# One written order for every engine in a two-pass attention and feed-forward kernel

## The reference

```
q = layernorm(x) @ Wq + bq ; k = ctx @ Wk + bk ; v = ctx @ Wv + bv      # split in 16 heads
scores = q k^T / sqrt(8), -1e9 where mask == 0 ; probs = softmax(scores)
x = x + (probs v) @ Wo + bo
h = gelu(bitlinear(layernorm(x), w1)) ; x = x + bitlinear(h, w2)
# bitlinear: rows rounded to 8 bits by their own maximum, weights to -1, 0, 1 times a scale
```

## Time and profile before

| | us |
|---|---|
| median of 3 runs | 1119.72 |
| lowest and highest run | 1116.97, 1119.76 |
| the profiled execution | 1116.7 |
| its span, first to last instruction | 1115.0 |
| granted TensorE clock over the span | 0.981 |

### The profile page before, as it was taken

The page is one execution under the profiler, slowest core; times in us unless marked ns, Lnnn a source line. Parts: engine busy times, 40 slices in busy tenths (PEclk is TensorE's granted clock), DMA queues, the critical chain, the costliest instruction groups (busy, mean ns, idle before and its releaser), DMA issues.

```text
span 1115.0 us, 29461 instructions
## 1 busy us (share of the span) xinstructions
PE 992.6 (89%) x10188; PEld 753.8 (68%) x10188; DVE 756.1 (68%) x1796; ACT 637.0 (57%) x1176; POOL 260.0 (23%) x414
## 2 busy tenths in 40 slices
PE   3588899999999999999999999999999999999994
PEld 1266676777767677776767777677776767777673
DVE  3767676776767776776777667676767767676664
ACT  1254456565575656557565665656566566666553
POOL 5402222222202222221222222122222211222200
PEclk9689999999999999999999999999999999999997
DMA  6553255453445545344554544455554444554300
GB/s 141 138 134 75 66 137 132 111 123 93 113 108 136 134 110 123 97 105 109 134 134 114 122 102 106 106 128 134 118 121 106 106 106 122 134 126 106 82 17 5
DMA packets 74985, 123.09 MB, mean 110 GB/s; under 512 B 6016, under 2 KB 58960, under 8 KB 74960
## 3 DMA queue, kind: packets, MB, share of 16 engines
q1 hardware_dynamic: 72649, 121.47, 45.7%
q10 hardware_dynamic: 2311, 1.29, 0.5%
HBM read 37.22 MB, written 0.92 MB: 34 GB/s over the span
## 4 chain that ended last, share of the span: by engine, by line
PE 53%; issue 15%; ACT 14%; DVE 12%; ACTq 3%; DMA 3%; SPq 1%; DVEq 0%
PE ps_v L810 10%; PE ps_p L704 8%; PE ps_s L767 8%; DVE seg_max L994 8%; ACT probs L602 7%; PE ps_s L772 7%; PE ps_p L708 6%; PE ps_p L723 5%; ACT k_hi L582 3%; PE ps_p L716 2%; PE ps_p L718 2%; ACTq L594 2%; PE ps_p L701 2%; ACT vals L586 2%; DMA ctx_sb<-in_ctx_dram 1%
## 5 line engine op out<-in xcount | busy, mean ns | idle before, releaser
L994 DVE TENSOR_REDUCE seg_max<-ps_p 128x1 f32<-128x500 f32 x672 | 422.8, 670 | 117.7 <-PE ps_p L723 114.8
L602 ACT ACTIVATE probs<-ps_s 125x448 f32<-125x448 f32 x768 | 367.7, 545 | 80.0 <-PE ps_s L772 75.3
L767 PE MATMUL ps_s<-qry,keys 121*125 121x448 f32 x768 | 292.9, 388 | 37.0 <-ACT probs L602 33.5
L772 PE MATMUL ps_s<-qry,keys 128*125 128x448 f32 x768 | 280.0, 371 | 0.0
L723 PE MATMUL ps_p<-keys,qry 120*128 120x500 f32 x576 | 243.3, 473 | 12.9 <-DVE k_lo L981 5.2
L586 ACT ACTIVATE vals<-ps_p 125x512 f32<-125x512 f32 x96 | 57.6, 600 | 279.9 <-PE ps_p L708 279.9
L767 PEld LDWEIGHTS ps_s<-qry,keys 121*125 121x125 f32 x768 | 140.8, 187 | 76.2 <-ACT probs L602 57.0
L810 PE MATMUL ps_v<-probs,vals 125*32 125x112 f32 x6144 | 168.0, 261 | 0.9 <-ACT probs L602 0.8
L810 PEld LDWEIGHTS ps_v<-probs,vals 125*32 125x32 f32 x6144 | 144.9, 110 | 30.3 <-issue 30.3
L723 PEld LDWEIGHTS ps_p<-keys,qry 120*128 120x128 f32 x576 | 109.6, 191 | 79.4 <-DVE seg_max L994 33.0
L772 PEld LDWEIGHTS ps_s<-qry,keys 128*125 128x125 f32 x768 | 142.2, 188 | 14.6
(11 more groups left out here) (123 smaller groups left out, 757.6 us busy)
## 6 DMA issues: line engine op xcount, KB each, us to landing
keys<-k_hi SPq DMA_DIRECT2D x128, 375.0 KB, 5.0
keys<-k_lo SPq DMA_DIRECT2D x64, 375.0 KB, 7.0
ctx_sb<-in_ctx_dram SPq DMA_DIRECT2D x31, 750.0 KB
keys<-keys SPq DMA_DIRECT2D x32, 328.1 KB
mask_sb<-in_mask_Bx1xSxS_ik_dram SPq DMA_DIRECT2D x31, 328.1 KB
out_dram<-x_rows SPq DMA_DIRECT2D x16, 56.0 KB, 1.6
ctx_sb<-in_ctx_dram ACTq DMA_DIRECT2D x1, 750.0 KB
x_rows<-in_x_dram SPq DMA_DIRECT2D x1, 672.0 KB, 11.6
```

The lines of the kernel that those rows point to most:

```text
L602: act.activation(probs[:, c % NP, h], ps_s[0:KC, (2 * c + h) % NS, 0:HC], ACT.Exp)\
L767: return pe.matmul(ps_s[0:KC, (2 * c + h) % NS, 0:HC], keys1[0:ONE + 1, p, h, c * KC:(c + 1) * KC], qry1[0:ONE + 1, p, h, :], start=start, ...
L772: return pe.matmul(ps_s[0:KC, (2 * c + h) % NS, 0:HC], keys2[:, p, h, c * KC:(c + 1) * KC], qry2[:, p, h, :], start=start, stop=not start)
L994: dve.tensor_reduce(seg_max[:, m, s:s + 1], bank[:, 0:SEG], AX.X, ALU.max)\
```

## The change

SLOTS and the sequences derived from it are replaced by one written list per kind of pass, which every engine walks, taking the words that concern it. A word is a piece with its number, or a job of one engine: own (values taken from ps_v), rows and hid (quantisation), sum (mask sum on ScalarE), some, bias, neg (turn_max), shift (place_shift), norm, abs, and k, the VectorE part of K.

- Each score half is a word of its own, with maxima, K, T and others between single halves.
- s0 s1 move from the end of the pass before to its own start.
- T1 and T2 stand apart from T0; K0 comes after S11; in the even pass V1, F0 and V2 stand before R0, and R0 before P2; in the odd pass R0 before P2 and V2 after.
- bias_mask stands before VectorE's copy of R instead of after it; find_some moves later; F0 moves from chunk 5 to near the end of the pass.
- VectorE's k part stands apart from K, mostly behind maxima or rows.
- The mask sum follows S9 (even) or T1 (odd).
- Banks go round in order, without the exception for G; S of the weight sum is called Z.

```diff
-SLOTS = [
-    [("T", 0), ("T", 1), ("T", 2), ("M", 0), ("D", 0), ("M", 1)],
-    [("M", 2)],
-    [("M", 3)],
-    [("M", 4), ("V", 0)],
-    [("M", 5), ("M", 6), ("M", 7)],
-    [("F", 0), ("M", 8), ("M", 9)],
-    [("K", 0), ("M", 10), ("M", 11)],
-    [("M", 12), ("V", 1)],
-    [("K", 1), ("M", 13), ("M", 14), ("M", 15)],
-    [("K", 2), ("M", 16), ("M", 17)],
-    [("M", 18), ("M", 19)],
-    [("M", 20), ("R", 0), ("V", 2)],
-]
+EVEN = order("""
+    own T0 s0 s1 f0 f1 S2 M0 D0 M1 S3 S4 T1 M2 S5 S6 M3 S7 M4 M5 S8 M6 S9 sum S10 S11 M7 M8 M9 K0 O0
+    rows P0 S12 k0 S13 k1 K1 V0 some S14 T2 M10 S15 rows1 S16 M11 K2 M12 k2 P1 S17 M13 M14 S18 S19
+    M15 S20 M16 M17 M18 S21 S22 M19 S23 M20 V1 F0 shift neg V2 bias R0 P2
+""")
+ODD = order("""
+    T0 own T1 s0 H0 sum s1 M0 M1 M2 f0 f1 S2 M3 T2 M4 M5 S3 S4 S5 M6 M7 M8 S6 D0 S7 hid G0 S8 K0 P0
+    S9 M9 hid1 K1 S10 S11 k0 M10 k1 S12 M11 M12 S13 hid2 S14 M13 V0 K2 k2 M14 hid3 S15 S16 M15 S17
+    P1 some M16 U0 M17 F0 S18 S19 Y0 M18 S20 M19 S21 M20 S22 neg S23 V1 shift bias R0 P2 V2
+""")
...
+LEAD = ["T0 T1 T2 M0 M1 some F M2 M3 K0 M4 M5 k0 M6 M7 K1 M8 M9 k1 M10 M11 K2 M12 M13 k2",
+        "M14 M15 M16 M17 M18 M19 M20 neg R shift V0 V1 V2 bias norm2"]
...
+    "first_even": with_more(EVEN, {"S5": "X1", "S7": "Q2", "S9": "Q3 abs", "S11": "B", "k1": "X2", "S21": "Q4", "S23": "Q5",
+                             "M20": "Z"}, ahead=(0, 1, 2)),
+    "last_even": ahead_only(EVEN, (-1, 0, 1)),
+    "last_odd": ahead_only(ODD, (-1, 0)),
...
-    if ("G", 0) in slots and len(slots) > 12:
-        at = slots.index(("G", 0))
-        own = (at + 7 - len(slots)) % NBANK
-        for n in range(at + 1):
-            bank[slots[n]] = (own + n - at) % NBANK
-        for n in range(6):
-            bank[slots[at + 1 + n]] = (own + 1 + n % 3) % NBANK
...
+            def score(bt, j):
+                b, k, p = bt
+                c, h = divmod(j, 2)
+                wait(pe, exp_done, 2 * NC * b + j - NS + 1)
+                first_pass(bt, c, h, True)
+                second_pass(bt, c, h, False).then_inc(scores_ready, 1)
```

More of the change, by code:

```diff
@@ L64 @@
[L64 to L79, removed]
@@ L82 @@
-PASS = {
[L83 to L92, removed]
+BANKED = "TKFVMRDOHGUYXQZWB"
@@ new lines, with with_more @@
+""")
[4 more added lines that the diff above has]
+""")
+def with_more(base, more, ahead=(-1, 0, 1, 2)):
+    at = {order(word)[0]: order(text) for word, text in more.items()}
+    out = []
+    for slot in base:
+        if AHEAD.get(slot[0], 0) in ahead and slot[0] not in OF_PAIR and slot[0] not in ("rows", "hid"):
+            out.append(slot)
+        out += at.get(slot, [])
+    return out
@@ L595, in place_shift, with exp @@
                     .then_inc(shift_placed[p], 16)
-            def exps(bt, c):
+            def exp(bt, j):
                 b, k, p = bt
[L599 to L603, removed]
-            def step(bt, how):
[L607 to L615, removed]
-                        sum_mask(later(bt, 2))
[L617 to L628, removed]
@@ L630, in _ @@
-            act.wait_ge(wk_loaded, 32)
[L631 to L639, removed]
+                c, h = divmod(j, 2)
+                if h == 0:
+                    wait(act, pv_done, NSEG * b + (c - NP) // NG + 1)
@@ new lines, in step @@
+            def step(bt, how):
+                for slot in PASS[how]:
+                    kind, n = slot
+                    if kind in ("S", "f"):
+                        exp(bt, n)
+                    elif kind == "sum":
+                        sum_mask(later(bt, 2))
+                    elif kind == "shift":
+                        place_shift(later(bt, 1))
+                    elif kind == "abs":
+                        sum_weights()
+                    elif kind in BANKED:
+                        take(slot, how, bt)
@@ L640, in _ @@
+            act.wait_ge(wk_loaded, 32)
+            step(batch(-1, 0), "open")
+            step(batch(-1, 1), "lead")
             steps(act, step)
-            take(("G", 0), "tail", batch(B // 2, 0))
+            step(batch(B // 2, 0), "tail")
         @block.tensor
@@ L814, in step @@
             def step(bt, how):
[L815 to L834, removed]
-                        fill(slot, how, bt)
[L836 to L843, removed]
+                for slot in PASS[how]:
+                    kind, n = slot
+                    if kind == "S":
+                        score(bt, n)
+                    elif kind == "s":
+                        open_score(bt, n)
+                    elif kind == "f":
+                        close_score(bt, n)
+                    elif kind == "P":
+                        values(bt, n)
+                    elif kind in BANKED:
+                        fill(slot, how, bt)
+            step(batch(-1, 0), "open")
+            step(batch(-1, 1), "lead")
             steps(pe, step)
-            for slot in FLAT["tail"]:
-                fill(slot, "tail", batch(B // 2, 0))
+            step(batch(B // 2, 0), "tail")
         @block.vector
@@ L973, in take @@
                 t = pair_of(st)
-                bank = ps_p[:, BANK[how][slot], :]
-                if kind == "K":
+                bank = ps_p[:, BANK[how]["K" if kind == "k" else kind, n], :]
+                if kind == "k":
                     dve.wait_ge(k_hi_ready, NSEG * b + n + 1)
@@ L1037, in take @@
                     wait_bank_full(dve, slot, how, st)
-                    if how == "even":
+                    if not isinstance(t, int):
                         rows = x_flat[:, bass.ds(t * D, D)]
@@ L1052, in take @@
                     wait_bank_full(dve, slot, how, st)
-                    if how == "odd":
+                    if not isinstance(t, int):
                         rows = x_flat[:, bass.ds(t * D, D)]
```

131 lines of the change are left out of this document (65 added, 66 removed).

## The result

| | before | after |
|---|---|---|
| median of four runs | 1118.35 us (1116.28 to 1119.76) | 1081.95 us (1079.08 to 1087.10) |
| ratio, 95% interval | | 0.9678 [0.9658, 0.9698] |
| profiled execution; its span | 1116.7; 1115.0 us | 1079.08; 1077.4 us |
| granted TensorE clock over the span | 0.981 | 0.969 |

The change makes the kernel 3.2% faster. Forecast were 1039 us and 7.2% off the 1119.7 shown: the direction is right, and less than half of the gain came. 1082 is the upper end of the range.

A forecast was written before the change was run, and what follows sets the result against it. TensorE, the fullest engine, had 9.3 of 64.74 us a pair not its own work. New pair: 55.4 + 3.0 seams + 0.4 + 0.3 + 0.5 = 59.6; 79.5 off 1116.7 gives 1037, stated as 1039; range 1008 to 1082.

The forecast's parts named there:

- the shift's way back: After R, f waits for the shift, back 3.0 us after R's start; cost 0.3 us a pair, bounds 0 to 1.1.
- the 1.52: TensorE's wait for the shift in the old last even pass, after R, V2 and two opening halves; forecast to mostly go.
- Mask sum and exponentials in the way: Start of passes: following mask sum and gelu with work needing neither removes most of 1.9 and 0.6 us a pair.
- (a): ScalarE's copies, exponentials and mask sum at pass start idle TensorE 0.8 us (even) and 1.1 (odd); transposes lose 0.6 a pair.
- R off the last reductions: Turning of the maxima near pass end waits for VectorE's last reductions; covering them by other work saves 1.1 us a pair.
- Maxima ahead of VectorE: Maxima issued in threes run ahead of VectorE, about 2.3 us a pair; single halves with maxima between remove most.
- F0 and GpSimd: Late F0 in the even pass delays GpSimd's query block, so the odd pass's M0 waits; 0.4 us a pair, bounds 0 to 1.0.
- Seams and margins: Late first starts where the kind of piece changes, 3.0 us a pair, plus 0.5 where margins under 0.7 are not kept.
- the 55.4: TensorE's own work in a pair of passes, in us, each kind of piece priced by distances between starts.
- VectorE did not become the bound: Rival: VectorE, with its fixed order and chained small operations, becomes the bound; about 1080 us, chance 0.14.
- TensorE full already: Rival: each weight load stands exposed beside its matmul, so order is free; time stays near 1119 us, chance 0.04.
- K0 on ScalarE: Slower rival: ScalarE's K0 copy waits for keys2, exponentials behind; decides from about 2.5 us per pass past cover; chance 0.08.

The follow-up runs named there:

- e8: e2 with T1 and T2 of the even pass moved beside T0, ahead of s and f; 1030.43 us, ratio to before 0.921.
- e2: The changed kernel's order, with SP holding the mask rows and the keys2 copies behind them until the shift has landed; 1039.70 us, ratio to before 0.930.
- e7: e2 with the even pass's mask sum behind S5 instead of S9; 1053.93 us, ratio to before 0.943.
- e12: e8 with P2 ahead of R in both kinds of pass, the bias ahead of both; 1044.92 us, ratio to before 0.934.
- e10: e8 with score halves in pairs in both kinds of pass; 1037.33 us, ratio to before 0.928.
- e11: e8 with VectorE's k0, k1 and k2 straight behind K0, K1 and K2 in both kinds of pass; 1069.24 us, ratio to before 0.956.
- e9: e8 with F0 of the even pass five score halves earlier, behind M16; 1033.24 us, ratio to before 0.924.
- e5: e2 with keys1's second copy also held on SP until the shift has landed; 1062.06 us, ratio to before 0.949, resting on three of four runs.
- e1: The changed kernel with the mask bias behind VectorE's copy of R in both kinds of pass; 1044.74 us, ratio to before 0.934.
- e6: e1 with T1 and T2 of the even pass moved beside T0, ahead of s and f; 1033.21 us, ratio to before 0.925.
- e3: e1 with P2 ahead of R again in both kinds of pass; 1052.64 us, ratio to before 0.942.

## Why less than half of the forecast gain came

**The failed step** is the term of the sum for "the shift's way back": "I take 0.3, bounds 0 and 1.1 a pair". It measured 2.96 a pair of idle time at f. I had taken "back 3.0 us after R's start" from the last even pass and set it against 3.8 and 3.5 us of cover. That row is read in the old order, where the shift (issued at 1050.40, landed 2.5 us later) stands 3.85 us behind the keys1 copies and 1.3 ahead of the mask rows:

```profile
1046.55 1.11 SPq L358 DMA_DIRECT2D keys<-k_hi  x2
1051.67 0.82 SPq L358 DMA_DIRECT2D keys<-keys  x1
```

I carried its 3.0 us over to an order in which both distances change. In the loop after the change the shift comes back 5.4 us (538.69 to 544.08) and 5.9 us (507.00 to 512.88) after R's start. The bias was in the sum as 1.07 us of VectorE's time; that it also releases a 328 KB copy and the keys2 copies behind it, and that R moved nearer to the last scores moves the shift nearer to two 375 KB copies, was not. The step listed who waits on the engine and not what goes out on the queues.

**How much it explains.** Pair forecast 59.6, measured 62.2: 2.6 too long, 14 x 2.6 = 36 of the 42 us between 1037 and 1079. Nine of the 36 are the falls of the clock, for which the sum has no term. They were seen only beside idle times of 1.7 us and more, mostly f's; that the idle time brings them is likely by that, but no run varied it alone, and eight pairs of after have the idle time and no fall. The pairs at full clock are at 61.5. With 2.96 - 0.3 = 2.7 of f's wait taken off, they would be at 58.9, 0.7 under the forecast. e8, without any wait at f in the loop, has pairs of 58.87, against 59.3 for the forecast without its 0.3. So the rest of the sum was 0.4 to 0.7 us a pair too long, and that e2, which changes only when SP's copies go out, runs in 1039.70, next to the 1039 forecast, is luck in part: it still has 1.2 us of f's wait. The other 6 us are outside these pairs. Of them the runs show the last even pass's wait for the shift, 2.62 us at 1013.89, where I had taken the 1.52 away.

**The other terms.**
- Mask sum and exponentials in the way: the gain is there, 0.96 a pair for the even pass's sum alone (e7), a little over the 0.8 that (a) has for the even pass. The odd pass's part and the gelu's were not priced by a run.
- R off the last reductions: forecast 1.1. The wait for the negated maxima (0.47 in each pass before) is gone in after. The 0.85 of e12 is near the 1.1 but isn't this wait: R does not wait for them there either, and T does for two copies. What R's place alone is worth against the old wait wasn't run.
- Maxima ahead of VectorE: forecast near 2.3 a pair, for which the rows shown hold one place of 0.64 only, and put down to single halves. e10 gives these 0.5 and e11 gives the later k_lo 2.8, for which I had no price: I had written it as something that comes late, where it is the largest relief. Together they are 3.3, more than the 2.3; the parts were not as I had them.
- F0 and GpSimd: forecast 0.4, measured 0.49 in the odd pass's M0; e9 shows that it can't be had back by itself.
- Seams and margins: never isolated. e8's 58.87 less the 55.4 and M0's 0.49 leaves 3.0 for them, where the sum has 3.5.

**The rivals.** VectorE did not become the bound; 1080 came out, but by another mechanism, and the waits tell them apart. TensorE full already falls: all 10188 loads and matmuls are the same and e8 is 7.9% shorter. The rule behind it is the Trainium skill's, that weight loads overlap "only when row_grp differs" (TensorE: Matmul & The Clock Gate, Part 3); this case's trace does not agree, with 0.41 us for two matmuls and two loads. K0 on ScalarE did not bite in after; it was real all the same: at 1.4 us a pass it costs nothing that TensorE's waits show (e8), at 3.0 a pass it costs 22 us (e5 against e2, with f's 1.2 us of wait saved), which bears out "from about 2.5 us past" only as to its kind, since some 2 us were the whole cover.

**Open.** Whether the mask rows or the keys2 copies behind them lengthen the flight was not separated: no run holds the one and not the other. Whether the 0.25 us by which e1 is slower than e2 per pair is the mask rows meeting the shift's tail or the bias standing behind it is open too. Why the even flight after the change varies between 5.1 and 5.9 us wasn't tried.

## What to carry to other kernels

When an instruction is moved, list for each semaphore that it raises which transfers are released by it, and where these stand against the small transfer that the critical engine waits for; a flight time read at one distance from the large transfers doesn't hold at another. If a small urgent transfer and large patient ones become ready together, hold the large ones until the small one has landed, but only as far as their own buffers allow: holding the mask rows and keys2 was worth 42 us here, and holding one keys1 copy as well gave 22 of them back. Compare pairs of passes at the same granted clock before a difference is put down to a wait. Price a part of a change only in a version from which the common wait has been removed.

## What the runs showed of the hardware

The flight of one 3.5 KB transfer goes by how long ago the two 375 KB copies of keys1 were issued, by the issue rows and the landings of these kernels:

| distance to the keys1 copies | flight |
|---|---|
| 1.4 us, and 328 KB more just ahead (after, even) | 5.1 to 5.9 us |
| 3.3 us, and 328 KB more just ahead (after, odd) | 4.2 us |
| 1.3 us, and 328 KB 1.0 us behind (e1, e6, even) | 4.65 and 4.7 us |
| 1.4 us (e2, e8, even) | 4.3 us |
| 1.4 us, one copy instead of two (e5, even) | 2.45 us |
| 2.8 us, and 328 KB 1.0 us behind (e1, e6, odd) | 2.85 us |
| 3.1 us (e3, e12, even) | 2.65 us |
| 3.3 us (e2, e8, odd) | 2.3 us |
| 3.8 to 3.9 us (before) | 1.84 and 1.93 us |
| 4.6 us (e3, e12, odd) | 1.84 us |

The distance is not all of it: in the last even pass of before, at 3.85 us, the flight is 2.51, and why wasn't looked into.

The shift was issued from ScalarE's queue and the copies from SP's, which did not keep them apart. That agrees with a line of the Trainium skill, "Trainium Kernel Development and Optimization", Key Constraints: transfers issued from SP, ScalarE and GpSimd run on the same 16 DMA engines and interleave, and issuing from several engines only saves issue time. No run issued the shift from SP's queue. Before e3 I had not expected that P2's 1.7 us between the copies and R come back almost whole: from e8 to e12 the even flight falls from 4.3 to 2.65 us.
